# Decay mixer of a two-layer network: another order of a batch's projections, transposes and x-projection

## The reference

```python
def _L1_attn_ref(x, W_in, conv_w, ln_gamma, ln_beta, W_xproj, A_param, D, W_out):
    xz = x @ W_in                                  # 256 -> 2 * 512
    xc, z = jnp.split(xz, 2, axis=-1)
    xc = conv_general_dilated(...)                 # 4 taps, one filter per channel, causal
    xc = _layernorm(silu(xc), ln_gamma, ln_beta)
    xp = xc @ W_xproj                              # 512 -> 33
    delta = clip(softplus(xp[..., :1]), 1e-06, 10.0)
    Bm, Cm = xp[..., 1:1 + n], xp[..., 1 + n:]     # n = 16
    A = -clip(softplus(A_param), 0.1, 10.0)
    decay = clip(exp(delta[..., None] * A[None, None]), 1e-06, 1.0)
    y = xc * einsum('bsn,bsin->bsi', Bm * Cm, decay) + xc * D
    return y * silu(z) @ W_out
```

## Time and profile before

| | us |
|---|---|
| median of 3 runs | 3203.21 |
| lowest and highest run | 3195.49, 3215.77 |
| the profiled execution | 3204.47 |
| its span | 3202.6 |
| StageD with its loads, about | 2108 to 2655 of the span |
| PE, DVE, ACT, POOL busy over the span | 2731.8, 2142.2, 1619.9, 1040.2 |
| mean granted PE clock | 0.937 |

### The profile page before, as it was taken

One profiled execution on the slowest core, in us unless ns is written; L12 is line 12 of the kernel. 1 busy time (PEld: TensorE's weight loads), 2 busy tenths in 40 slices (PEclk: granted clock), 3 DMA queues, 4 the chain that ended last, 5 costly groups with the idle time before them and its releaser, 6 DMA issues.

```text
span 3202.6 us, 40169 instructions
## 1 busy us (share of the span) xinstructions
PE 2731.8 (85%) x13591; PEld 1655.3 (52%) x13654; DVE 2142.2 (67%) x3854; ACT 1619.9 (51%) x2421; POOL 1040.2 (32%) x714
## 2 busy tenths in 40 slices
PE   7778887787765789999887999957988888999999
PEld 4445554454443355555554666634444435666666
DVE  1689898888886667777533222236887895777776
ACT  3778778777871245555441111137787881111111
POOL 0788888888881221111101000012112000100000
PEclk9899999999876899999998999977998999999999
DMA  3588887788884665555513000020000002000000
GB/s 113 116 170 148 180 170 159 154 174 174 149 192 94 174 174 98 88 89 86 85 54 143 24 24 24 17 52 14 7 7 11 3 1 60 7 14 7 7 7 14
DMA packets 122344, 262.93 MB, mean 82 GB/s; under 512 B 14784, under 2 KB 76992, under 8 KB 120480
## 3 DMA queue, kind: packets, MB, share of 16 engines
q0 software_dynamic: 28000, 134.89, 20.7%
q1 hardware_dynamic: 94144, 125.47, 17.2%
HBM read 135.40 MB, written 131.20 MB: 83 GB/s over the span
## 4 chain that ended last, share of the span: by engine, by line
PE 49%; issue 7%; ACT 6%; DVE 5%; DMA 1%; POOL 0%; POOLq 0%; ACTq 0%; DVEq 0%
PE PS L2376 7%; PE PS L1677 6%; PE PS L2394 6%; PE PS L1972 4%; PE PS L1699 3%; PE PS L1340 2%; ACT Z L2114 2%; PE PS L2014 2%; PE PS L1319 2%; PE PS L1322 2%; PE PS L1267 2%; PE PS L1297 2%; PE PS L1996 1%; PE PS L1366 1%; PE PS L1272 1%
## 5 line engine op out<-in xcount | busy, mean ns | idle before, releaser
L856 POOL TENSOR_TENSOR Z<-Z 128x1024 f32<-128x1024 f32 x256 | 646.5, 2737 | 127.4 <-DVE Z L757 78.6
L764 DVE TENSOR_TENSOR_SCAN Z<-PS,Z 128x1024 f32<-128x1024 f32 x256 | 576.3, 2274 | 21.6 <-ACT PS L684 11.8
L535 PE MATMUL PS<-Z 128*128 128x128 f32 x2048 | 305.8, 296 | 124.2 <-DVE Z L764 50.0
L535 PEld LDWEIGHTS PS<-Z 128*128 128x128 f32 x2048 | 251.2, 152 | 254.7 <-issue 82.2
L684 ACT ACTIVATE PS<-Z 128x511 f32<-128x511 f32 x512 | 332.8, 687 | 61.8 <-DVE Z L764 59.9
L1436 ACT ACTIVATE Z<-PS 128x512 f32<-128x512 f32 x320 | 189.0, 596 | 269.9 <-PE PS L1322 257.6
L2427 ACT ACTIVATE Z<-PS 128x512 f32<-128x512 f32 x144 | 85.9, 597 | 410.4 <-PE PS L2376 410.4
L696 ACT ACTIVATE Z<-PS,Z 128x512 f32<-128x512 f32 x378 | 246.1, 684 | 81.2 <-PE PS L535 73.3
L2376 PE MATMUL PS<-Z 128*128 128x512 f32 x576 | 272.3, 598 | 7.9 <-DVE Z L2509 7.1
L1529 DVE TENSOR_REDUCE Z<-PS 128x1 f32<-128x512 f32 (+2 forms) x384 | 182.5, 507 | 121.4 <-PE PS L1298 118.5
L2114 ACT ACTIVATE Z<-Z 128x2048 f32<-128x2048 f32 x128 | 252.6, 1998 | 15.3 <-PE PS L2014 9.2
(11 more groups left out here) (293 smaller groups left out, 4888.8 us busy)
## 6 DMA issues: line engine op xcount, KB each, us to landing
sums<-Z POOLq DMA_DIRECT2D x112, 768.0 KB, 8.3
Z<-rows_b SPq DMA_DIRECT2D x128, 256.0 KB, 4.7
Z<-scr SPq DMA_DIRECT2D x256, 128.0 KB, 6.3
rows_n<-in_L_ffn_expert_wv POOLq DMA_DIRECT2D x32, 528.0 KB, 7.8
scr<-Z SPq DMA_DIRECT2D x32, 384.0 KB
Z<-Z POOLq DMA_DIRECT2D x14, 768.0 KB, 7.6
Z<-in_L_ffn_expert_wv SPq DMA_DIRECT2D x4, 2048.0 KB, 15.1
Z<-sums SPq DMA_DIRECT2D x7, 768.0 KB, 6.5
```

The source lines that it names most:

```text
L535: ins = e.transpose(self.turned[i % 2][:, c * 128:(c + 1) * 128], self.h(k, c // 2)[:, c % 2, i * 128:(i + 1) * 128], ident)
L764: e.tensor_tensor_scan(h, a, h, 0.0, ALU.mult, ALU.add).then_inc(s["scan"], 1)
L856: e.tensor_tensor(self.h(k, f), self.du[b % 2][:, 2 * f:2 * f + 2, :], b3(self.Bs[k % 2], 1, [128, 2, 512]), ALU.mult).then_inc(s["hin"], 1)
```

## The change

Only the table `PLAN` changes: a batch's 54 preparation steps stay the same, and so do the waits of each. The table of batch 0, `START`, stays as it is; but since batch 1's preparation runs between batch 0's last places, the order changes there too.

- Lifts 0 and 1, 3 and 4, 5 and 6 stand in pairs with no sum between them; lift 7 is one place later, behind the sum's last quarter.
- The evacuation of lift 7 stands in the gate activation's place, so behind the `wout` there.
- Flip 0 and flip 1 stand in two places. The four `xn` stand in one, so `xn` 3 comes behind `minus` and a scale.
- Taps 1 and 2 stand in one place, taps 3 one place later.
- `xproj` is one place behind `xf`, `pj` and `soft` one place behind that, in one place with `clip` and `rep`.

```diff
     PLAN = (
-        (("stats",),), (("rstd",), ("minus",)), (("norm",),), (("flip", 0), ("flip", 1)),
-        (("flipped", 0), ("flipped", 1), ("lift", 0)), (("lifted", 0), ("lift", 1)), (("taps", 0), ("lifted", 1)),
-        (("lift", 2),), (("lifted", 2), ("taps", 1), ("lift", 3)), (("lifted", 3), ("lift", 4)),
-        (("taps", 2), ("lifted", 4), ("lift", 5)), (("lifted", 5), ("lift", 6)),
-        (("taps", 3), ("lifted", 6), ("lift", 7)), (("lifted", 7),), (("silu",),),
-        (("turnx", 0), ("turnx", 1), ("turnx", 2), ("turnx", 3)), (("stats2",),), (("rstd2",), ("xn", 3)),
-        (("xn", 0), ("xn", 1), ("xn", 2)), (("back", 0), ("back", 1), ("back", 2), ("back", 3)),
-        (("xf", 0), ("xf", 1), ("xf", 2), ("xf", 3), ("xproj",)), (("zx",), ("pj",), ("soft",)),
-        (("clip",), ("rep",)), (("scalars",),))
+        (("stats",),), (("rstd",), ("minus",)), (("norm",),), (("flip", 0),), (("flip", 1), ("flipped", 0), ("flipped", 1)),
+        (("lift", 0), ("lift", 1)), (("lifted", 0), ("taps", 0), ("lifted", 1)), (("lift", 2),),
+        (("lift", 3), ("lift", 4), ("lifted", 2)), (("taps", 1), ("taps", 2), ("lifted", 3)), (("lifted", 4),),
+        (("lift", 5), ("lift", 6)), (("lifted", 5),), (("taps", 3), ("lifted", 6), ("lift", 7)), (("lifted", 7), ("silu",)),
+        (("turnx", 0), ("turnx", 1), ("turnx", 2), ("turnx", 3)), (("stats2",),), (("rstd2",),),
+        (("xn", 0), ("xn", 1), ("xn", 2), ("xn", 3)), (("back", 0), ("back", 1), ("back", 2), ("back", 3)),
+        (("xf", 0), ("xf", 1), ("xf", 2), ("xf", 3)), (("xproj",),), (("pj",), ("soft",), ("zx",), ("clip",), ("rep",)),
+        (("scalars",),))
```

## The result

The changed kernel takes 3183.02 us (median of 6 runs, 3175.93 to 3195.24), the kernel before 3202.61 beside it (6 runs, 3195.49 to 3215.77): ratio 0.9937, 95% interval 0.9919 to 0.9954. A second set of runs gave 0.9938 (0.9917 to 0.9958).

A forecast was written before the change was run, and what follows sets the result against it. No engine is full: a 61.6 us period is ACT's half, then PE's, so only a shorter hand-over counts. 6 x 1.44 + 0.6 + 1.3 = 10.5 us off 3203.2 gives near 3193, range 3179 to 3208.

The forecast's parts named there:

- rival C: Faster by the clock: the half-clock lift behind the x-projection vanishes, 8.9 us below the forecast, about 3184; chance 0.12.
- The hand-over, 6 x 1.44: End of PE's half: lift 7 behind the sum, its evacuation behind wout, silu starts earlier; gain 1.44 us a batch.
- The x-projection and the flips, net 0: Behind xf: flip 1 and the x-projection one place later leave rep, the scalars and the waiting grow unmoved; net 0.
- Pairs, net 0: PE's lifts in pairs: the same set of work takes the same time in either order, so nothing is gained or lost.
- The grow behind the pair 3, 4: ACT: the grow waiting for the sum quarter behind lift 4 waits one lift longer, about 1.9 us, until 2372.2.
- PE's idle ahead of turning xc: PE's 1.53 us wait for the gate activation falls to 0.1, under 0.3 as a sign of being right.
- Scales beside GpSimd's products: DVE scale steps inside GpSimd's four gating products slow by up to 4.06 us; 4.3 us of room hides it, net 0.
- rival B: Slower by DVE and GpSimd: the 4.06 us reaches taps 3, silu 1.9 us later a batch, about 3214; chance 0.08.
- The clock "as before": Lift behind the x-projection: its half-clock cost of 1.49 us kept unchanged; losing it (-8.9) or paying twice (+4.7) only in range.
- The signs of "wrong": Rep or scalars later against the gate activation, silu waiting for taps 3, or mean granted clock off 0.91 by over 0.02.
- Ends: Ramp and tail of the batches: 0.6 us gained at the first grow, 1.3 us in the last batch.

The follow-up runs named there:

- the second trace: The changed kernel run again with nothing edited, for another trace: 3180.22 against 3199.9, ratio 0.9938.
- the filled kernel: Changed kernel plus eight unused 128 x 256 matmuls in PE's 4.5 us wait for a scale on DVE, ahead of the flips: ratio 0.9928.
- four partial tables: Kernel before with lift 7 and its evacuation moved, 0.9998; with flips and x-projection later, 1.0005; changed kernel with x-projection back, 0.9994; without pairs, 0.9987.
- the hand-over alone: Kernel before with only lift 7 one place later and its evacuation in the gate activation's place: 3203.18 against 3203.93, ratio 0.9998.
- the fastest order: Changed kernel with xf, flip 1, both flipped, x-projection, lifts 0 to 3, rep and scalars one place earlier: 3175.99 against 3206.23, ratio 0.9897.
- my kernel for that: Changed kernel with xf and flips one place earlier and the x-projection in halves, lifts 0 and 1 and a sum quarter between them: ratio 0.9978.

## Why the prediction was right, and where not

The sign and the range held; the forecast of 10.5 us was half of the 19.6 measured. The time that came, 3183, is that of rival C (3184), but not by C's way: half-clock lifts became fewer and did not vanish, and the order gained more than forecast. That the two together make C's number is luck. Step by step:

- *The hand-over, 6 x 1.44: right in size.* Lift 7's end to the table load, less the sum: 1.42 shorter. Table load behind lifted 7 behind wout, nothing waiting. The prediction gave this gain to the two moves of lift 7; the runs show that they alone bring 0.93 of it (1.77 from lift 7's end to the table load, in place of 1.28) and 1.1 a period (60.51 against 61.63, and 61.00 against 62.03). The last 0.49 is there in all kernels in which the evacuations of lifts 5 and 6 stand a place later, with the pairs or without; by ACT's rows that place is what frees it, but no run moves them alone.
- *The x-projection and the flips, net 0: right.* 59.55 us a period with them back, 59.47 as changed, each with one stretch.
- *Pairs, net 0: mis-sized.* At full clock the table's own gain is 2.16 a period, 0.7 more than forecast. My start-to-start counting took each lift as 1.91 and each sum quarter as 1.00, and held "the same set of work" to take the same time in any order. It does not: two lifts side by side take 3.53 to 3.63 (2359.64 to 2363.17 in the trace after), two quarters 1.85 (2363.17 to 2365.02), against 3.82 and 2.00 apart. The run without pairs puts this at 0.5 a period. The other 0.2 is on PE too, and it is there with lift 7's moves alone (1.12 less 0.93). By PE's rows 0.24 of the 0.7 lies ahead of rep and 0.48 between rep and lift 7's end.
- *The grow behind the pair 3, 4, which waits about 1.9 longer: right.* It waits 2.15 where it waited 0.43, and nothing behind it is late.
- *PE's idle ahead of turning xc, 1.53 to under 0.3: right.* It has none.
- *Scales beside GpSimd's products, hidden: right.* 3.1 us longer for the four, where up to 4.06 was allowed, and the copy still waits for PE. By the rule of the Trainium skill (SBUF — State Buffer, "Who interferes with whom") a DVE tensor_scalar in a two-port mode and a GpSimd operation exclude each other; the trace agrees, with 4.74 against 1.63 us. It cost nothing, and rival B did not happen. Taps 3 ends at 2368.04, 0.2 ahead of the table load and 1.4 ahead of the activation behind it.
- *The clock "as before": the step that was off.* The prediction gave the half-clock lift vanishing a chance of 0.12, as an alternative to the gain in order. It priced the stretch at 1.49, the lift alone; with the end of the x-projection it is 1.70. It also read 0.89 beside 63.21 as bearing on what sets the clock; those two numbers show only what a lower clock costs. It is neither kept nor gone: six of six periods have a stretch on the lifts before, one of six in the first trace after and three in the second. The clock takes 348.43 - 6 x 57.78 = 1.8 and 353.34 - 6 x 57.78 = 6.7 us of the six periods, against 374.29 - 6 x 59.94 = 14.7 before. So of 25.9 us in the periods 13 is order (6 x 2.16) and 13 the clock; by the second trace 13 and 8 of 21.
- *The signs of "wrong".* Rep is not later: it starts 35.09 us behind the table load, where it was 37.03; 1.70 of the 1.94 is the clock. Silu does not wait for taps 3. The mean granted clock in the periods, 0.91 before, is 0.93 and 0.92 after; the bound of 0.02 that I set was reached once and not passed. It was a poor sign: the cost lies in where the half clock falls, not in how much there is, as the filled kernel shows (1.00 against 0.94, same period).
- *Ends: small and uneven.* Last batch 0.8 for 1.3. Ramp 3.2 for 0.6 in the first trace, but 50.73 against 50.99 in the second, 0.3; so the 3.2 is not the order's.

Why did four partial tables (0.9998, 1.0005, 0.9994, 0.9987) gain nothing, when the order alone is worth 2.16? The mean period of them is 61.7 to 62.5. Like against like, the hand-over gains 1.1 a period and the table without pairs 0.9 (60.72 against 61.63), the later x-projection alone loses 0.7 by its wait for flipped 1; the third, with the x-projection back, gains 2.08 (59.55 against 61.63) in the one period that can be compared. What is gained, stretches in other periods take back. What is not settled: why the pattern of clean periods and stretches repeats from period to period (five of 57.8; three of 61.63; 60.6 and 62.3 in turn) and then shifts in another execution, and so why the changed kernel has fewer. It was seen that it does; a single profile of each of the partial kernels can't tell its usual pattern. Also open is whether the fastest order would give 56.15 us a period without its five stretches, for my kernel for that had a fault.

## What to carry to other kernels

Count a move of queue places to the next wait, not to the sum of durations: here lift 7's 1.4 us was real, but 0.5 of it needed another move, and 8 of 21 us in one trace and 13 of 25.9 in the other came from a side (the clock behind a row of narrow matmuls) that the rows had shown and that I wrote off as constant. When a periodic kernel has periods of two lengths, find what makes the long ones before costing a change; compare like with like, since a partial version can gain its microsecond and hand it back. Doing a step of an order alone is no test of its share when the steps free each other.

## What the runs showed of the hardware

- A row of 32 matmuls of 128x33 on end can be followed by half clock on the 512-wide matmuls behind it, with no gap in PE's rows (3.40 us start to start for a lift against 1.89). The old order has it in 6 of 6 periods, and so do the hand-over alone, the new order without pairs and the one with the x-projection back; the new order has it in 1 and 3 of 6, the later x-projection alone in 3, the fastest in 5, the one with the filled wait in 2. With two 256-wide matmuls in the middle of the row it is 0 of 6 (old order), 0 of 6 (new order) and 1 of 6 (hand-over); with flip 1 and a sum quarter there, 0 of 6. Each count is from one trace. The Trainium skill (TensorE: Matmul & The Clock Gate, "Part 1") has the clock follow how busy the array has been. The trace neither confirms nor contradicts this: PE's rows show no gap where the clock fell to 0.50, and no run here shows what the chip counted.
- Half clock on work behind which PE waits for another engine anyway is free: 57.77 us with a granted clock of 1.00 or 0.94. On the flips it cost 1.2 to 1.6 us, on the lifts 1.7.
- The same program has periods of 57.77, 59.44 and 61.14 us in one execution, with exactly the same instructions. The difference is where half clock falls.
